# Later due times for the output projection and the gate work of the middle attention layer

## What is computed

```
x = x + cross_attention_0(layernorm(x), ctx, tau, delta)      # 16 heads, 120 keys
x = x + ffn_0(layernorm(x))     # inside: h = z + self_attention(layernorm(z)), 16 heads, 256 keys
                                #         h + expert[argmax(layernorm(h) @ gate_w)](layernorm(h))
x = x + cross_attention_1(layernorm(x), ctx, tau, delta)
x = x + ffn_1(layernorm(x))     # 128 small experts, each takes the best token of its column
```

## Time and profile before

| | us |
|---|---|
| median of three runs | 880.48 |
| the profiled execution | 880.48 |
| its span | 878.6 |
| TensorE busy | 706.8 |
| VectorE busy | 472.7 |
| ScalarE busy | 363.5 |
| GpSimd busy | 233.3 |
| start of the scores of n = 8 (span time) | 201.6 |
| end of the last `pv` of n = 15 | 387.1 |
| first expert matmul | 421.8 |

### The profile page before, as it was taken

The page is one execution under the profiler, slowest core; times in us unless marked ns, Lnnn a source line. Parts: engine busy times, 40 slices in busy tenths (PEclk is TensorE's granted clock), DMA queues, the critical chain, the costliest instruction groups (busy, mean ns, idle before and its releaser), DMA issues.

```text
span 878.6 us, 16001 instructions
## 1 busy us (share of the span) xinstructions
PE 706.8 (80%) x5896; PEld 537.5 (61%) x5896; DVE 472.7 (54%) x1207; ACT 363.5 (41%) x671; POOL 233.3 (27%) x312
## 2 busy tenths in 40 slices
PE   2648789888988888854799999993687887788898
PEld 1435566655665665533798989992454565456775
DVE  3147567767777878554121222223276777654575
ACT  1516466545664554530223242220335556534323
POOL 0403234333342331121211121003525444332000
PEclk9769899989999999995799999997569999976999
DMA  4886583865546663351955666621638463061202
GB/s 160 102 111 154 90 117 68 108 87 85 81 83 91 87 86 122 135 189 51 345 189 158 219 172 180 178 109 52 100 50 135 67 98 51 27 261 48 98 13 85
DMA packets 59305, 101.96 MB, mean 116 GB/s; under 512 B 7187, under 2 KB 49619, under 8 KB 54069
## 3 DMA queue, kind: packets, MB, share of 16 engines
q1 hardware_dynamic: 57357, 95.83, 48.8%
q0 software_dynamic: 1872, 5.11, 3.0%
HBM read 55.38 MB, written 7.21 MB: 71 GB/s over the span
## 4 chain that ended last, share of the span: by engine, by line
PE 56%; DVE 13%; ACT 8%; DMA 7%; issue 5%; POOL 5%; SPq 5%; ACTq 0%; DVEq 0%; POOLq 0%
PE PS L849 9%; PE U L860 8%; PE MB L679 8%; PE MB L776 6%; SPq L1629 4%; PE U L752 4%; PE MB L932 3%; DVE nma L1209 3%; PE MB L711 3%; PE PS L734 2%; PE MB L695 2%; DMA QKa<-mTa 2%; PE MB L942 2%; DMA ctx<-in_ctx 1%; DMA Qb<-mTb 1%
## 5 line engine op out<-in xcount | busy, mean ns | idle before, releaser
L1209 DVE TENSOR_REDUCE nma<-MB 128x2 f32<-128x512 f32 (+1 forms) x192 | 122.4, 671 | 51.3 <-PE MB L711 51.1
L1034 ACT ACTIVATE Pa<-PS 128x1024 f32<-128x1024 f32 (+1 forms) x96 | 97.8, 1025 | 65.4 <-PE PS L734 64.1
L849 PE MATMUL PS<-mzT,mw 128*128 128x128 f32 x736 | 88.7, 280 | 3.7 <-DMA mw<-in_mw 2.9
L711 PE MATMUL MB<-QKa 99*128 99x120 bf16 (+1 forms) x512 | 71.0, 254 | 24.7 <-DVE nma L1209 10.6
L849 PEld LDWEIGHTS PS<-mzT,mw 128*128 128x128 f32 x736 | 86.5, 197 | 4.6 <-DMA mw<-in_mw 3.6
L860 PE MATMUL U<-mw,mdT 128*128 x368 | 83.6, 380 | 5.0 <-DVE mdT L1381 2.3
L1389 DVE TENSOR_TENSOR yt<-U,mb 128x256 f32<-128x256 f32 x23 | 9.8, 425 | 128.8 <-PE U L860 128.8
L860 PEld LDWEIGHTS U<-mw,mdT 128*128 128x128 f32 x368 | 68.1, 190 | 14.2 <-issue 5.9
L711 PEld LDWEIGHTS MB<-QKa 99*128 99x128 bf16 x512 | 39.5, 102 | 54.0 <-DVE nma L1209 17.0
L1471 POOL TENSOR_TENSOR mv<-mv,vec 128x2 f32<-128x2 f32 (+1 forms) x40 | 30.6, 766 | 131.8 <-DVE mv L1168 79.2
L734 PE MATMUL PS<-QKa 101*128 101x256 bf16 (+1 forms) x384 | 59.3, 279 | 7.1 <-DMA QKa<-mTa 7.1
(11 more groups left out here) (203 smaller groups left out, 1306.2 us busy)
## 6 DMA issues: line engine op xcount, KB each, us to landing
mw<-in_mw SPq DMA_DIRECT2D x31, 1024.0 KB, 5.7
QKa<-spa SPq DMA_DIRECT2D x144, 128.0 KB, 4.6
Qb<-spb SPq DMA_DIRECT2D x48, 128.0 KB, 4.6
Oa<-Uba SPq DMA_DIRECT2D x16, 256.0 KB, 3.1
v<-in_v SPq DMA_DIRECT2D x1, 4096.0 KB, 13.8
v<-in_v SPq DMA_DIRECT2D x4, 1024.0 KB, 12.1
W<-in_W SPq DMA_DIRECT2D x3, 1280.0 KB, 7.6
yb<-yt SPq DMA_DIRECT2D x23, 128.0 KB, 1.7
```

The lines of the kernel that those rows point to most:

```text
L711: i = e.matmul(b[:, keys * j:keys * j + keys], Q[0:99, h0 + j, 128 * qt:128 * qt + 128], K[0:99, h0 + j, 0:keys], start=True, stop=True)
L849: i = e.matmul(ps[:, 128 * f:128 * f + 128], w[:, k, 128 * f:128 * f + 128], zz[:, k, :], start=k == 0, stop=k == 1)
L1034: e.activation(p[0:keys, :], ps[0:keys, :], ACT.Exp, scale=0.25).then_inc(sems["exp"], 1)
L1209: e.tensor_reduce(A.nm[qt][:, h0:h0 + heads], b[:, 0:heads * keys].rearrange("p (h s) -> p h s", h=heads), AX.X, ALU.max, negate=True).the ...
```

## The change

Two tuples of due times are changed. For the self attention `p2` is due at 1.82 instead of 1.72 batches. The six groups of the gate work are each due 0.03 to 0.13 batches later. Nothing else is changed: the same instructions are issued, in another order.

```diff
-T_PROJECT = ((1.44, 1.5, 2.1, 2.56), (1.28, 1.33, 1.6, 1.72), (1.35, 1.4, 1.9, 2.05))
+T_PROJECT = ((1.44, 1.5, 2.1, 2.56), (1.28, 1.33, 1.6, 1.82), (1.35, 1.4, 1.9, 2.05))
 EARLY_KEYS = {4: 16, 9: 18}
-T_AFTER = (1.75, 2.0, 2.2, 2.35, 2.6, 2.85)
+T_AFTER = (1.88, 2.07, 2.25, 2.4, 2.63, 2.88)
```

## The result

The kernel after took 888.15 us (median of 4 runs, 886.53 to 891.41) against 879.54 us before on the same chips (877.42 to 881.03). The ratio is 1.0104, 95% interval 1.0066 to 1.0143: **slower by 1.0%**, where 878.2 us had been forecast and the range ended at 883.0.

The account below looks back on a forecast made before the run. TensorE and VectorE were taken as close in the self attention, TensorE waiting ahead of `p2` for VectorE's `Oa`. Late gain -7.9, early periods +1.5 net of old low clock, hold +0.8, low clock +3.3: -2.3, so 878.2 us, range 873.5 to 883.0.

Parts of the forecast that it names:

- the hold of VectorE by GpSimd: Periods of n = 10 and 11: `nb` to `y` slowed beside a GpSimd instruction, +0.8 us (0 to 1.7 for both).
- the low clock: Periods of n = 10 to 13: two of four TensorE waits bring the 1.2 GHz level, +3.3 us (0 to 6.6).
- the main wait: Self attention, n = 11: TensorE's 1.66 us wait ahead of `p2` moves to the eighth `mx`, as 1.7 us.
- the late gain: Periods of n = 14 and 15 (-6.65 us) and the earlier reciprocal behind the last scores (-1.4, `gs` +0.2): -7.9 us.
- first stretch: Third `mx` of n = 11 to `gt` of n = 12, holding all periods with maxima from `p2` of n = 8: +5.6 us.
- the order, n = 9 to 13: Periods with maxima: the new order alone, without low clock, makes them longer by 0.9 to 1.1 us each, +4.8 us.
- second stretch: `gt` of n = 12 to `p1` of n = 15, periods without maxima and tail; -7.9 us forecast to the first expert matmul.
- The bound and the place: Self attention: TensorE and VectorE nearly equally busy (22.4 and 20.6 of 25.4 us in n = 11); TensorE waits ahead of `p2`.
- `nb` to `y`: Self attention: took 1.57 instead of 0.73 us beside a GpSimd instruction; expected again in n = 10 and n = 11.
- more than two as a sign of being wrong: Self attention, 228 to 360 us: more than two stretches of low clock would show the prediction wrong.
- The fourth rival: n = 14 and 15: the chain from `p2` to `gt` ends last, late gain becomes a wait; +2.8, 883.3 us, chance 0.15.
- The third: Periods with maxima: low clock in all four waits and both `nb` blocked; +1.9, 882.4 us, chance 0.10.

Follow-up runs that it names:

- e5: The kernel after with three GpSimd instructions of the self attention (L1480, L1487, L1507) cut to 8 columns: 882.01 us, ratio 0.9975.
- e6: The kernel before with the same three GpSimd instructions (L1480, L1487, L1507) cut to 8 columns: 877.6 us, ratio 0.9952.
- e4: The kernel before with the new due times for batches 8 to 12 alone: 901.66 us, ratio 1.0291.
- e1: The kernel before with only `p2`, `xy`, `na 2`, `nb 2` (and `hs`) later, gate work unmoved: 895.5 us, ratio 1.0190.
- e7: The kernel after with GpSimd's `xy` addition (L1507) alone cut to 8 columns: 887.39 us, ratio 1.0074.
- e11: The kernel after with `p2` one slot later still (due 1.88), behind `mh`, a `mx` and `gs`: 899.32 us, ratio 1.0230.
- e2: The kernel before with only the gate work `gl`, `gr`, `gs` later, `p2` unmoved: 870.03 us, ratio 0.9891.
- e3: The kernel before with the new due times for batches 13 to 15 alone (and `gl`, `gr`, `gs` of 12): 868.42 us, ratio 0.9883.
- e9: The kernel before with `gr` and `gs` alone later, `gr` behind `p1`: 872.22 us, ratio 0.9873.
- v2_best: The kernel before with `gr` and `gs` later everywhere and `gl` later from batch 12 on: 866.72 us, ratio 0.9859.

## Why the prediction was wrong

Two terms of the sum were far too small: the hold of VectorE by GpSimd (+0.8) and the low clock (+3.3, as much as before had). The place and kind of the main wait and the late gain were right.

**The sum of the first stretch, taken apart.** At a clock of 0.91 a stretch of 138.0 us has lost at most 138.0 × 0.09 = 12.4 us to the low level; before it was 116.1 × 0.03 = 3.5, in e5 126.4 × 0.08 = 10.1, in e6 116.0 × 0.03 = 3.5. Without that after has 125.6, before 112.6, e5 116.3, e6 112.5 us. So

| | forecast | measured | from |
|---|---|---|---|
| the order, n = 9 to 13 | +4.8 | +3.8 | e5 - e6 |
| VectorE held by GpSimd | +0.8 | +9.3 | after - e5; VectorE busy 100.5 and 91.3 |
| low clock | 3.3 there, 3.3 gone | +8.9 (+3.1 in e4) | 12.4 - 3.5 (6.6 - 3.5) |
| first stretch | +5.6 | +21.9 | 138.0 - 116.1 |
| second stretch | -7.9 to the first expert matmul | -8.3 | 32.4 - 40.7 |

Each stretch is of one execution, and the clock is shown in steps of 0.01, which is 1.4 us of 138. The accounting holds where it can be tested: e4, with the same order at another clock, is 132.1 - 6.6 = 125.5 us without the low level, after 125.6. The lengths without low clock are thus safer than the share of the clock, which is 6.6 us in one execution of this order and 12.4 in another. The ratios of whole runs, 1.0104 and 0.9975 for after and e5, differ by 1.3%, some 11 us, in line with the stretches.

- **The bound and the place were right.** VectorE and TensorE are close in the periods with maxima, and the wait of `p2` became one of the eighth `mx`. The order term was 1 us too large.
- **The late periods were right**: no wait for `Oa`, the reciprocal at the landing of `La`. `gt` of n = 13 waits 0.88 us while n = 15 has its scores (0.9 forecast), and the last wait for `nb` 2, behind the last scores, is 1.43 us, of which I had not spoken.
- **The step that failed is the hold by GpSimd**, put at +0.8 us and measured at 9.3. My replay used each instruction's own time of before, and corrected that only for `nb` to `y`, "0 to 1.7 for both". In the new order it was not `nb` that met GpSimd but the chain of `gl`, a step of `gr`, and L1220; `nb` to `y` fell from a mean of 710 to 431 ns. The rule that I cited from the Trainium skill ("SBUF — State Buffer", "Who interferes with whom") has a second half that I passed over: a VectorE instruction with two SBUF inputs contends with a GpSimd instruction that reads SBUF. The runs agree with it: L1264, L1270, L1299 and L1220 have two SBUF inputs and are held to the end of the GpSimd instruction, and with GpSimd short, in e5, their means are 173 to 241 ns. My error was to carry over times from a place where GpSimd was quiet. The upper end of that term should have been each such instruction times what is left of a GpSimd instruction of 1.2 us.
- **The low clock was the second step that failed.** I took two of four waits as followed by it, with 6.6 us as the upper end. In the profiled execution it followed all four, where before it was three of six, once for some 7 us on end, and it came twice more behind waits of 1.35 us that the replay did not price: six places, where I had named more than two as a sign of being wrong, and at most 12.4 us. The four were waits of 1.55 to 2.39 us with small ones ahead (0.81, 0.29, 0.21), in all longer than the 1.66 of before; and where `pv` and `vp` run at half the clock, VectorE idles longer (4.37 us ahead of L1197 in n = 11, 0.61 before). e5, without holds, still has a clock of 0.92, so the low clock does not need the holds. It goes with the late `p2`: in the first stretch the clock is 0.91 to 0.95 in the six profiled kernels that have it (after, e1, e4, e5, e7, e11) and 0.97 to 1.00 in the six that don't (before, e2, e3, e6, e9, v2_best). What exactly brings it was not settled.
- **The fourth rival** (late gain lost to `gt`) didn't happen. The third, "low clock in all four, both `nb` blocked", came nearest in kind, and was still 6 us short: its price for the holds was 1.7 and for the low clock 6.6. By the stretches of the two profiled executions the change cost 13.6 us (21.9 less 8.3), by the medians 8.6, so even this distance depends on how much low clock an execution has.
- **A slip in the rivals**: the three waits of 1.66 us (266.40, 294.67, 320.10) lie in the periods of n = 10 to 12; "n = 9 to 11" are the batches whose `p2` waits.

Half of the change is a gain. The part that helps is the later gate work, `gr` behind `p1` above all; the late `p2` takes away its cover, brings `xy` beside L1220, and comes with more low clock.

## What to carry to other kernels

A replay with measured durations holds only as long as each VectorE instruction meets the same GpSimd instructions: list, for every small VectorE instruction with two SBUF inputs that moves, what GpSimd does then. When two things are moved together, ask whether one was the cover of the other: here the ranks later alone gave -1.3%, the projection later alone +1.9%. In a stretch near 80% busy on two engines, price a wait of 2 us with the low clock behind it, and take it as likely; compare two orders by the lengths of a stretch without the low clock, since its place changes from one execution to the next.

## What was not expected of the hardware

- A VectorE tensor_tensor on 128x2 elements took 0.99 us instead of 0.16 beside a GpSimd tensor_tensor of 1.17 us; tensor_reduce (L1209, 0.68 us, at 364.64 in after) kept its time beside a GpSimd tensor_tensor of 1.28 us (364.57), and so did L1220 at 364.55, which started 0.02 us ahead of it and took 0.17 us.
- Holds can cost nothing where TensorE has other work: the first stretch of e2 has 5.0 us more of VectorE time than that of before and is 2.0 us shorter, at the same clock of 0.97.
- A clock of 0.67 over 44.6 us in e11, with TensorE idle for 6.3 us of it, against 0.95 in after with 6.2 us of 32.4: the idle time alone doesn't tell how long the low level lasts.
